# Mixture-of-experts tail of a fused transformer block: who computes the low halves of the expert weights, and when

## The reference, cut to what matters

```python
probs = jax.nn.softmax(jnp.einsum('btd,de->bte', x, gate_w), axis=-1)
expert_weights, expert_indices = jax.lax.top_k(probs, 2)
expert_weights = expert_weights / expert_weights.sum(-1, keepdims=True)
for i in range(8):
    wi = jnp.where(expert_indices == i, expert_weights, 0.0).sum(-1)
    h = jax.nn.silu(x @ w1[i]) * (x @ w3[i])        # 256 -> 1024
    out = out + (h @ w2[i]) * wi[..., None]         # 1024 -> 256
```

## Time and profile before

| | us |
|---|---|
| median of 3 runs | 903.18 (902.73 to 903.85) |
| span of the profiled execution | 894.1 |
| TensorE busy | 697.5 (78%) |
| VectorE busy | 575.9 (64%) |
| ScalarE busy | 386.0 (43%) |
| GpSimd busy | 292.0 (33%) |

### The profile page before, as it was taken

One profiled execution on the slowest core, in us unless ns is written; L12 is line 12 of the kernel. 1 busy time (PEld: TensorE's weight loads), 2 busy tenths in 40 slices (PEclk: granted clock), 3 DMA queues, 4 the chain that ended last, 5 costly groups with the idle time before them and its releaser, 6 DMA issues.

```text
span 894.1 us, 19056 instructions
## 1 busy us (share of the span) xinstructions
PE 697.5 (78%) x4439; PEld 466.6 (52%) x4483; DVE 575.9 (64%) x1409; ACT 386.0 (43%) x795; POOL 292.0 (33%) x372
## 2 busy tenths in 40 slices
PE   2999998995474579157741899989998989889992
PEld 2677776663222357146630455655665656556662
DVE  5588889998598945278878455455545464564441
ACT  1455554444553235335521454445444454454330
POOL 4333333331000110064431225263536353653331
PEclk9999999999697579655555899999999999999997
DMA  8100000000000011331127052525252425432123
GB/s 252 31 12 12 12 12 12 6 0 1 1 0 1 0 48 47 118 113 31 29 95 241 19 167 30 149 42 167 30 153 41 123 71 148 123 88 30 24 31 106
DMA packets 45843, 58.41 MB, mean 65 GB/s; under 512 B 13496, under 2 KB 39416, under 8 KB 45272
## 3 DMA queue, kind: packets, MB, share of 16 engines
q1 hardware_dynamic: 38328, 47.79, 16.7%
q0 software_dynamic: 7488, 10.31, 7.3%
HBM read 145.90 MB, written 11.80 MB: 176 GB/s over the span
## 4 chain that ended last, share of the span: by engine, by line
PE 46%; DVE 21%; issue 15%; POOL 8%; DMA 3%; ACT 3%; DVEq 2%; POOLq 1%; ACTq 1%; SPq 0%
PE psum L958 16%; PE psum L980 6%; PE psum L694 5%; POOL region L636 3%; PE psum L971 3%; PE psum L701 2%; PE psum L680 2%; DVE region L1449 2%; PE psum L858 2%; PE psum L714 1%; DVE region L1297 1%; DVE region L1295 1%; PE psum L733 1%; PE psum L685 1%; PE psum L851 1%
## 5 line engine op out<-in xcount | busy, mean ns | idle before, releaser
L958 PE MATMUL psum<-region 128*128 x897 | 209.5, 381 | 18.3 <-POOL pause_p L638 7.3
L958 PEld LDWEIGHTS psum<-region 128*128 128x128 bf16 x936 | 91.7, 98 | 117.8 <-issue 29.1
L980 PE MATMUL psum<-region 128*128 x936 | 109.0, 273 | 6.1 <-DVE region L1793 4.7
L1763 DVE TENSOR_TENSOR region<-psum,region 128x512 f32<-128x512 f32 x78 | 53.9, 691 | 72.9 <-ACT region L1199 70.0
L980 PEld LDWEIGHTS psum<-region 128*128 128x128 bf16 x936 | 90.5, 98 | 19.3 <-issue 8.8
L521 POOL TENSOR_TENSOR region<-region,head_mask 128x1024 f32<-128x1024 f32 x32 | 60.1, 1898 | 121.9 <-DVE region L1291 121.9
L1199 ACT ACTIVATE region<-psum 128x512 f32<-128x512 f32 x78 | 46.5, 596 | 118.5 <-PE psum L958 118.4
L606 POOL TENSOR_TENSOR pause_p<-minus_half 128x1 f32<-128x1 f32 x37 | 7.2, 194 | 186.2 <-DVE next_token L1779 185.4
L694 PE MATMUL psum<-region 128*128 128x512 f32 x128 | 63.6, 620 | 3.5 <-POOL region L521 3.5
L618 POOL DMA_INDIRECT sum_dram<-region,tok_idx x39 | 62.0, 1589 | 6.2 <-issue 5.9
L1793 DVE TENSOR_TENSOR region<-psum,region 128x1024 bf16<-128x1024 f32 x39 | 47.7, 1223 | 17.5 <-ACT region L1207 17.5
(11 more groups left out here) (294 smaller groups left out, 1377.3 us busy)
## 6 DMA issues: line engine op xcount, KB each, us to landing
region<-in_L_ffn_w SPq DMA_DIRECT2D x117, 1024.0 KB
region<-in_ctx SPq DMA_DIRECT2D x48, 128.0 KB, 2.1
region<-neg_max_dram SPq DMA_DIRECT2D x4, 1024.0 KB, 7.9
xrow_dram<-region SPq DMA_DIRECT2D x1, 2080.0 KB, 7.8
x_sb<-in_x SPq DMA_DIRECT2D x4, 512.0 KB, 6.5
sum_dram<-x_sb SPq DMA_DIRECT2D x1, 2048.0 KB, 7.5
region<-in_L_ffn_w_down SPq DMA_DIRECT2D x1, 704.0 KB, 8.7
region<-in_L_ffn_w_gate SPq DMA_DIRECT2D x1, 640.0 KB, 8.8
```

The source lines that it names most:

```text
L958: last = mm(psum[:, 2 * f + n, :], (xT_lo if xl else xT_hi)[:, p, k, :], weights_at(place, wl, n, k * F1 + f * FH, FH), start=(i == 0), st ...
L980: last = mm(psum[:, 7, 0:D], (hT_lo if hl else hT_hi)[:, f, :], weights_at(place, wl, 2, f * D, D), start=(i == 0), stop=(i == 3 * (F1 // ...
L1763: tt(h_d[:, p, f * FH:(f + 1) * FH], psum[:, 2 * f + 1, :], sil_d[:, f, :], ALU.mult).then_inc(h_d_ready, 1)
```

## The change

All low halves are computed by VectorE. GpSimd's `weights_low` is deleted. In VectorE's `tile_step` three calls now stand in a row at the end, behind `weighted(t-1)`: n = 0 for tile t+3, n = 1 for t+2, n = 2 for t+1, so that the three matrices of a new expert fall to three successive tiles. ScalarE's casts are put in the same order at its tile's end, w1 three tiles ahead instead of two. SP issues the load of w1 five tiles ahead instead of four. The loops are two tiles shorter, with more tiles peeled off behind them.

```diff
--- before.py
+++ after.py
@@ -466,20 +466,22 @@
                 load_part(n, 2, 0)
             load_part(0, 3, 1)
             load_part(1, 3, 1)
+            load_part(0, 4, 0)
 
             def load_step(t, p, inner=False):
 
+                if inner or t + 5 < NT:
+                    load_part(0, t + 5, 1 - p, inner)
                 if inner or t + 4 < NT:
-                    load_part(0, t + 4, p, inner)
                     load_part(1, t + 4, p, inner)
                 if inner or t + 3 < NT:
                     load_part(2, t + 3, 1 - p, inner)
 
             load_step(0, 0)
-            with sp.Fori(0, (NT - 5) // 2) as i:
+            with sp.Fori(0, (NT - 7) // 2) as i:
                 load_step(2 * i + 1, 1, inner=True)
                 load_step(2 * i + 2, 0, inner=True)
-            for t in range(NT - 4, NT):
+            for t in range(NT - 6, NT):
                 load_step(t, t % 2)
             sp.wait_ge(sum_added, 16 * NT)
             sp.dma_start(out.rearrange("b p d -> (b p) d"), sum_dram[0:B * P, :]).then_inc(out_stored, 16)
@@ -623,25 +625,10 @@
             gather_rows(0, 0)
             gather_rows(1, 1)
 
-            def weights_low(t, p, inner=False):
-
-                place = pool.value_load(tile_info[0:1, 1, bass.ds(t, 1)], min_val=0, max_val=(SLOTS - 1) * SLOT)
-                new = pool.value_load(tile_info[0:1, 2, bass.ds(t, 1)], min_val=0, max_val=1)
-
-                pool.wait_ge(part_low[0], t)
-
-                pool.wait_ge(part_high[0], t + 1)
-                nc.gpsimd.tensor_tensor(pause_p[:, 2:3], minus_half[:, 0:1], minus_half[:, 0:1], ALU.add)
-                with pool.If(new > 0):
-                    nc.gpsimd.tensor_tensor(expert_w[:, bass.ds(place + 3 * PART, PART)], stage[:, p, 0, :],
-                                            expert_w[:, bass.ds(place, PART)], ALU.subtract)
-                nc.gpsimd.tensor_tensor(pause_p[:, 3:4], minus_half[:, 0:1], minus_half[:, 0:1], ALU.add).then_inc(part_low[0], 1)
-
             def step_d(t, p, inner=False):
                 gather_rows(t + 2, p, inner)
                 if inner or t >= 1:
                     add_rows(t - 1, 1 - p, inner)
-                weights_low(t + 2, p, inner)
 
             pool.wait_ge(info_ready, 1)
             for t in range(3):
@@ -1227,13 +1214,13 @@
                 silu_d(t, 0)
                 if inner or t >= 1:
                     h_high(t - 1)
-                if inner or t + 2 < NT:
-                    weights_high(0, t + 2, p, pair + 2, inner)
                 if not inner and t == 0:
                     x_high(1, 1)
                 silu_d(t, 1)
                 if inner or 0 < t < NT - 1:
                     x_high(t + 1, 1 - p)
+                if inner or t + 3 < NT:
+                    weights_high(0, t + 3, 1 - p, pair + 2 + p, inner)
                 if inner or t + 2 < NT:
                     weights_high(1, t + 2, p, pair + 2, inner)
                 if inner or t + 1 < NT:
@@ -1246,11 +1233,13 @@
             weights_high(2, 0, 0, 1)
             weights_high(0, 1, 1, 1)
             weights_high(1, 1, 1, 1)
+            weights_high(0, 2, 0, 2)
             tile_step(0, 0, 0)
-            with act.Fori(0, (NT - 3) // 2) as i:
+            with act.Fori(0, (NT - 5) // 2) as i:
                 tile_step(2 * i + 1, 1, i, inner=True)
                 tile_step(2 * i + 2, 0, i + 1, inner=True)
-            tile_step(NT - 2, 1, (NT - 2) // 2)
+            for t in range(NT - 4, NT - 1):
+                tile_step(t, t % 2, t // 2)
             tile_step(NT - 1, 0, (NT - 1) // 2)
             h_high(NT - 1)
 
@@ -1801,11 +1790,13 @@
                 hidden_d(t, p, 1)
                 if inner or 0 < t < NT - 1:
                     x_low(t + 1, 1 - p)
-                if inner or t + 2 < NT:
-                    weights_low(1, t + 2, p, inner)
                 route_of(t, p, loads, inner)
                 if inner or t >= 1:
                     weighted(t - 1, 1 - p)
+                if inner or t + 3 < NT:
+                    weights_low(0, t + 3, 1 - p, inner)
+                if inner or t + 2 < NT:
+                    weights_low(1, t + 2, p, inner)
                 if inner or t + 1 < NT:
                     weights_low(2, t + 1, 1 - p, inner)
 
@@ -1814,14 +1805,15 @@
             weights_low(2, 0, 0)
             weights_low(0, 1, 1)
             weights_low(1, 1, 1)
+            weights_low(0, 2, 0)
             tile_step(0, 0, 1)
             tile_step(1, 1, 1)
             tile_step(2, 0, 2)
-            with dve.Fori(1, (NT - 3) // 2) as i:
+            with dve.Fori(1, (NT - 5) // 2) as i:
                 tile_step(2 * i + 1, 1, i + 1, inner=True)
                 tile_step(2 * i + 2, 0, i + 2, inner=True)
-            tile_step(NT - 2, 1, NT // 2)
-            tile_step(NT - 1, 0, NT // 2 + 1)
+            for t in range(NT - 4, NT):
+                tile_step(t, t % 2, t // 2 + 1)
             h_low(NT - 1)
             weighted(NT - 1, 0)
```

## The result

| | before | after |
|---|---|---|
| median, same chip (4 runs each) | 903.51 (902.73 to 904.66) | 937.21 (935.38 to 939.22) |
| profiled execution: span | 894.1 | 935.9 (device time 937.77) |

The change makes the kernel slower: ratio 1.0368, 95% interval 1.0347 to 1.0388. On a second chip the same pair gave 936.63 against 898.41, ratio 1.041 [1.0381, 1.0439].

What follows compares the result with a forecast made beforehand. The prediction took VectorE's sequencer, with three blocks in its ring, as the bound after the change: loop +34.0, start +3.0, tail +0.6 make +37.6 on the 894.1 us span; with 9.1 outside it, 941 us, range 917 to 953.

Steps and rivals of the forecast that it cites:

- the ring: VectorE's serial round per tile, down_d, weighted, blocks, hidden_d, h_low: from 6.8 or 7.1 us to 10.45 or 10.62.
- VectorE's sequencer becomes the bound: In tiles where all three calls are made, VectorE's round of 10.45 or 10.62 us exceeds TensorE's 9.2.
- The sign of a missed term: VectorE's first block waiting for ScalarE's cast would show a term left out of the forecast; no size given.
- A skipped block costs 1.65 to 1.8 us: On VectorE's sequencer, one skipped weights_low block takes 1.65 us in plain form, 1.8 with address arithmetic.
- rival B: Skipped blocks on VectorE cost ScalarE's 1.33 us each: slightly slower, 911 us; chance 0.10.
- Ordinary tiles 10.45 and 10.62 in turn, 337.1 us for 32: Loop of tiles 3 to 34: odd tiles 10.45 us, even ones 10.62, 337.1 in sum against 317.1 before.
- Subtractions: +14 us: Uncovered subtraction time on VectorE in the loop: 0.7 for w1, 0.75 for w3, 12.5 for w2.
- Rival C: TensorE's clock falls to 1.2 GHz part of the time from 1.3 us idle a tile: about 1030 us; chance 0.03.
- Start +3.0, tail +0.6: Outside the loop: down_d(0) 1.9 us later, two tiles before the loop +1.1, tile 35 +0.6.
- the 9.1 us outside the span: Time between the profiled span of 894.1 us and the median of 903.2, added to the forecast span of 931.7.
- A: Table reads hide in VectorE's wait for down_d, expert changes lose 19.1 us: faster, about 885.6 us; chance 0.12.
- a block under 1.2 us: Skipped block on VectorE: the cost below which the even round stays at TensorE's 9.2 us.

Runs made afterwards that it cites:

- e3: Kernel before plus one pair of table reads, results unused, at the end of VectorE's tile: 904.04 us, ratio 1.005 to before.
- e4: Kernel before plus three pairs of table reads, results unused, at the end of VectorE's tile: 970.83 us, ratio 1.0783 to before.
- e7b: Changed kernel, VectorE's blocks kept but never entered, all 24 subtractions left out, TensorE reading high halves for low: 919.73 us, ratio 1.0173 to before.
- a0: Changed kernel without an edit, run again on a second chip: 936.63 us, beside 898.41 for before.
- e0: Kernel before without an edit, timed and profiled a second time: 897.8 us, profiled span 897.7.
- e1: Changed kernel with VectorE reading the place of the weights only inside the branch: 902.38 us, ratio 1.0043 to before.
- e10: Changed kernel with new-weights flag and place packed in one number, one register read per VectorE and ScalarE block: 886.03 us, ratio 0.9798 to before.

## Why the prediction was right, and where it was not

The forecast was 941 us, with 0.75 on the ring; measured 937.21. By its steps:

1. *VectorE's sequencer becomes the bound.* Right. `down_d` waits for `h_low` in 36 tiles, VectorE's gaps ahead of the pauses are "issue", and e3 and e4 show the threshold with reads alone. As forecast, `hidden_d` hardly waits for ScalarE in the loop (once, 0.2 us). The sign of a missed term, a wait of a block for ScalarE's cast, came once, 2.5 us at 495.9, ahead of the loop.
2. *A skipped block costs 1.65 to 1.8 us.* Right as a sum: `weighted` to `hidden_d` came out at 5.83 in an even tile against 5.80 (2.31, 1.8, 1.65, 0.04), and at 5.67 in an odd one against 5.63 (1.98, twice 1.8, 0.05), in after and in e7b. Single blocks are less even, 1.56 and 1.89; none is near ScalarE's 1.33, on which rival B rested. Each sits on two register loads of 0.31 us and the register arithmetic around them. In all tiles of after, VectorE's sequencer:

```profile
L1725 DVEq TENSOR_LOAD <-tile_info x117: 298/308/665, 478.4 to 906.2; - x117
...
L1726 DVEq TENSOR_LOAD <-tile_info x117: 297/305/327, 479.3 to 906.9; - x117
```

3. *Ordinary tiles 10.45 and 10.62 in turn, 337.1 us for 32.* Right: 10.3 to 10.7 in after, mostly 10.5 and 10.65 in turn, and 336.8 for 32 tiles in e7b, which has nothing else in its loop.
4. *Subtractions: +14 us.* Too small, by 4.2 in after and 2.9 in a0. In after w2's seven tiles exceed e7b's 10.53 by 1.9 us each, 13.5 where the prediction had 12.5. Two tiles behind a slow `down_d` take 11.93 and 11.95 us instead of 10.62 and 10.30 in a0, where those `down_d` are at full speed: 3.0 us. What is left for w1 and w3 is 1.7, where the prediction had 1.45. The slower clock is a term that it left out of the sum; but a0 has only one slow `down_d` in its loop (4.48 us, behind 2.32 of idle time), and e0, the kernel before, has one too (4.47, below), so it isn't the change's alone. Rival C had a falling clock, but from 1.3 us of idleness in every tile and over the whole loop. That did not come: in e7b, with 1.2 to 1.7 us of it in every tile, the granted clock of the loop is 1.00, though TensorE reads other data there.
5. *Start +3.0, tail +0.6.* `down_d(0)` came at 509.55, +1.4 where +1.9 was predicted (from 3.2 us for two blocks of 1.65, which make 3.3), and `down_d(2)` at 529.52 against 526.78, +2.7. The tail was 51.4 us behind `down_d(34)` against 50.2, +1.2. But e0 has `down_d(0)` at 509.92 and a tail of 51.5, so these two differences are within what the kernel before varies by. The two tiles from `down_d(0)` to `down_d(2)` are firmer: 20.0 us against 18.6 in both profiles of before, +1.4 where +1.1 was predicted.
6. *The span, and what lies around it.* The step "with the 9.1 us outside the span" was wrong. The device time of every run that shows both is 1.7 to 2.2 us above its span (937.77 and 935.9 here). The 9.1 us are mostly a difference between executions: a span of 894.1 us makes about 896 of device time, while the timed runs gave 903. In e0's group single executions of before have spans from 893.9 to 900.8 us, and medians differ by chip, so the profiled one was quick, or ran on another chip; which of the two, no run shows. On span the change was 41.8 us in the first pair of profiles and 37.5 in a0 and e0 (935.2 - 897.7), against 37.6 predicted; in medians it was 33.7 on one chip and 38.2 on the other. So the loop and its blocks are confirmed closely, but that the total came within 4 us is in part luck: the 9.1 us that were added to the span are 7 too many, and in after the subtractions' 4.2 us work against that.

*Rivals.* A (885.6 us) was wrong for this change. Its condition, a block under 1.2 us, is what brings the ordinary tiles back to TensorE's pace, in e1 as in e10. It isn't enough for A's time: e1's blocks take 0.95 to 1.03 us, and it takes 902.38 us, 0.4% over before. e10 with 1.03 takes 886.03 (0.9798 of 904.39), but there the reads of the subtracting tiles and of ScalarE are cheaper too. In neither do table reads run during the wait for `down_d`, as A had it, so that the two times nearly agree is partly luck. What the Trainium skill ("GPSIMD Engine Reference", section "Engine selection") advises, two-input elementwise work to VectorE, is thus sound for the subtraction (2.29 against 4.64 us) and pays here once what stands around it is cheap, as in e10; the rule prices the instruction and not the registers that decide on it.

Open: which of e10's cheaper reads gave its gain over e1; why the kernel before takes 898 to 899 us on two chips and 904 elsewhere, when its two profiled executions, of 894.1 and 897.7 us of span, have nearly the same loop, 317.1 and 317.7; and why only some of the tiles with equal idle times are followed by a slower clock. e10 was timed beside before on one chip only.

## What to carry to other kernels

Before moving conditional work to an engine, follow the ring of waits that this engine is part of, and count in it every register read and branch, whether the work is done or skipped; busy time shows none of it. Then make the condition cheap, for the tiles that skip and for those that don't: one packed number in place of two reads, on VectorE and ScalarE, turned a change of +3.7% into one of -2%. When a block is moved forward on one engine, check what it then waits for on the engine that feeds it.

## What the runs showed of the hardware beyond that

- A table read costs VectorE's sequencer some 0.6 to 0.7 us, of which 0.31 is the load: a skipped block with two takes 1.56 us, and with one 0.95 (even tiles of after and e1). The Trainium skill ("DMA: Bandwidth & Descriptors", section "Latency and other measured facts") gives `tensor_load` a floor of about 600 ns; the 117 loads of L1726 in after, from on-chip memory, are at half of that (297 to 327 ns), and here the measurement decides.
- TensorE's granted clock fell for single `down_d` in a loop otherwise at full speed, in both kernels: behind idles of 3.0 us (after), 2.3 (a0), 2.1 and 2.0 (e1, 4.36 and 4.47 us for a `down_d` of 2.8), 1.2 to 1.4 (e3), and in e0, the kernel before, behind only 0.41 us, with 1.35 ahead of the transposes before it (granted clock 0.66 from 767.5 to 772.5). Other idles of 3.0 us were followed by a `down_d` of 2.83. None fell in the loop of the first profile of before, of e10 (at most 1.06 there) or of e7b (1.2 to 1.7 in every tile). So the idle time right ahead does not decide it in these runs; what does is open. `down_d` of e3, then of e0:

```profile
633.53 4.48 PE L980 MATMUL psum<-region 128*128 x24 [1.20 <-DVE region L1793]
```

```profile
767.59 4.47 PE L980 MATMUL psum<-region 128*128 x24 [0.41 <-issue]
```

- What stands behind a subtraction in the sequencer's order is hidden as far as it fits into the 2.29 us; what stands ahead of it is not. In after, behind w1's subtraction, that is one block of two reads, and the third block's pause still comes 1.24 us later (626.74 to 627.98). In e10 the branch's end and the whole next block behind w3's subtraction pass within 0.01 us of each other as it ends:

```profile
616.84 2.29 DVE L1734 TENSOR_TENSOR region<-region 128x2048 f32 x1 [0.34 <-issue]
...
619.08 0.06 DVE L1736 MEMSET pause_d<- 128x1 f32 x1
619.09 0.06 DVE L1731 MEMSET pause_d<- 128x1 f32 x1
619.09 0.06 DVE L1736 MEMSET pause_d<- 128x1 f32 x1
```
